# Class words of a graph network kernel: 10 of 25 groups in the setup, 15 one a step, and a loop that begins at step 19

## The reference

```
A1 = adj * (y @ y.T)                      # edges within one class
x  = layernorm(x + 0.9 * (A1 / rowsum(A1)) @ x + 0.1 * h0)
w  = tanh(adj * adj), the 350 largest of each row kept
h2 = tanh(x @ W_proj + b_proj)
x  = layernorm(x + relu(w @ (h2 @ W_gcn) + b_gcn))
```

## Time and profile before

| what | us |
|---|---|
| three runs | 461.50, 460.99, 461.31; median 461.31 |
| the profiled execution | 461.15 |
| its span, first to last instruction | 459.4 |
| TensorE busy | 429.9 (94%) |
| VectorE busy | 379.3 (83%) |
| ScalarE busy | 266.5 (58%) |
| GpSimd busy | 162.2 (35%) |

### The profile page before, as it was taken

How to read it: one execution, slowest core, us unless ns; L and a number is a source line. 1 busy time by engine, 2 the same in 40 slices (tenths; PEclk the granted TensorE clock), 3 DMA queues, 4 the chain that set the end, 5 groups by cost and what they waited for, 6 DMA issues and landing times.

```text
span 459.4 us, 15106 instructions
## 1 busy us (share of the span) xinstructions
PE 429.9 (94%) x5104; PEld 381.6 (83%) x5104; DVE 379.3 (83%) x1363; ACT 266.5 (58%) x363; POOL 162.2 (35%) x311
## 2 busy tenths in 40 slices
PE   3669999999999999999999999999999999999994
PEld 2447998888988888888888987788888888888883
DVE  5988999999999999999999987786666666666663
ACT  4987999998999999999999963840000000000000
POOL 3012443544455544455544453132221221221222
PEclk9986999999999999999999999999999999999998
DMA  8999999999999999999999500000000000000000
GB/s 267 409 414 420 393 411 411 392 414 409 421 415 422 423 422 417 423 421 423 417 424 422 221 2 2 8 17 11 17 16 12 17 15 13 17 14 15 17 13 26
DMA packets 25518, 108.49 MB, mean 236 GB/s; under 512 B 5097, under 2 KB 15490, under 8 KB 15490
## 3 DMA queue, kind: packets, MB, share of 16 engines
q1 hardware_dynamic: 25490, 108.14, 58.4%
HBM read 105.57 MB, written 2.56 MB: 235 GB/s over the span
## 4 chain that ended last, share of the span: by engine, by line
PE 77%; DVE 10%; issue 6%; ACT 3%; DMA 2%; POOL 2%; POOLq 0%; DVEq 0%; SPq 0%
PE acc L576 65%; PE words L514 6%; DVE a_bits L862 3%; DMA a_rows<-in_adj_dram 2%; DVE turned L949 2%; PE feat_acc L643 2%; PE proj_acc L656 1%; PE xnt_acc L635 1%; ACT count_out L743 1%; ACT x_parts L729 1%; DVE z_high L1017 1%; POOL rstd L454 1%; DVE stats L1030 1%; DVE mean_var L1035 0%; DVE f_parts L982 0%
## 5 line engine op out<-in xcount | busy, mean ns | idle before, releaser
L576 PE MATMUL acc<-x_parts,turned 128*128 128x257 f16 x1560 | 189.2, 277 | 4.5 <-DVE turned L949 3.5
L743 ACT ACTIVATE count_out<-a_rows,ones 128x2688 bf16<-128x2688 f32 (+1 forms) x80 | 190.2, 2377 | 0.5
L576 PEld LDWEIGHTS acc<-x_parts,turned 128*128 128x128 fp8e4 x1560 | 152.3, 99 | 27.3 <-issue 4.9
L576 PE MATMUL acc<-f_parts,turned 128*128 128x256 f16 x1520 | 165.3, 271 | 1.8 <-DVE f_parts L982 1.8
L576 PEld LDWEIGHTS acc<-f_parts,turned 128*128 128x128 fp8e4 x1520 | 147.1, 98 | 18.9 <-DVE f_parts L982 1.3
L862 DVE TENSOR_SCALAR a_bits<-a_rows 128x2688 bf16<-128x2688 f32 (+1 forms) x80 | 116.6, 1457 | 1.9 <-DMA a_rows<-in_adj_dram 1.5
L451 POOL TENSOR_TENSOR var_eps<-mean_var,consts 128x1 f32<-128x1 f32 x79 | 18.4, 233 | 258.5 <-DVE mean_var L1035 129.6
L949 DVE TENSOR_SCALAR turned<-a_words 128x320 uint16 (+1 forms) x304 | 66.2, 231 | 48.7 <-PE acc L576 48.7
L454 POOL TENSOR_TENSOR rstd<-var_eps,consts 128x1 f32<-128x1 f32 x79 | 87.3, 1105 | 6.2
L949 DVE TENSOR_SCALAR turned<-same_class 128x320 uint16<-128x320 uint16 x313 | 71.4, 254 | 0.1
L514 PEld LDWEIGHTS words<-pack,a_bits 128*128 128x128 bf16 (+1 forms) x1600 | 51.6, 97 | 9.5 <-DVE a_bits L862 7.5
(11 more groups left out here) (134 smaller groups left out, 295.6 us busy)
## 6 DMA issues: line engine op xcount, KB each, us to landing
a_rows<-in_adj_dram SPq DMA_DIRECT2D x39, 1344.0 KB, 7.5
a_rows<-in_adj_dram SPq DMA_DIRECT2D x39, 1156.0 KB, 8.0
out_dram<-xn SPq DMA_DIRECT2D x39, 64.0 KB, 1.5
h_rows<-in_L_gnn_h_dram SPq DMA_DIRECT2D x19, 128.0 KB, 7.7
xs<-in_x_dram SPq DMA_DIRECT2D x3, 640.0 KB, 10.0
xs<-in_x_dram SPq DMA_DIRECT2D x1, 512.0 KB, 9.0
y_nat<-in_L_gnn_y_dram SPq DMA_DIRECT2D x1, 304.0 KB, 3.6
a_rows<-in_adj_dram SPq DMA_DIRECT2D x1, 84.0 KB
```

The source lines that it names most:

```text
L576: mm = pe.matmul(acc[par][0:m, used], bits, parts[:, b, used], start=first and b == blocks[0], stop=last and b == blocks[-1])
L743: act.activation(count_out[0:m, 0:w], a_rows[par][h][0:m, 0:w], ACT.Relu, bias=ones[0:m, 0:1], scale=-HUGE, accum_out=col).then_inc(s_coun ...
```

## The change

Groups 10 to 14 leave step 1 (on TensorE, ScalarE and VectorE). Groups 10 to 24 are made one a step in steps 2 to 16 instead of groups 15 to 24 in steps 2 to 11. Since group g is now made in step g - 8, VectorE copies the even groups in steps 2, 4, ..., 16 and ScalarE the odd ones in steps 4, 6, ..., 16. `FIRST` becomes 19, so that steps 13 to 18 are written out. Two waits are new: TensorE's transpose of step 5 waits for the copies of groups 6 to 9, whose banks it shares, and `mask` of block 16 waits for groups 13 and 14.

```diff
-    FIRST = 13
+    FIRST = 19
...
-        EARLY_GRAMS = 3 * GRAMS
+        EARLY_GRAMS = 2 * GRAMS
...
                 same_class_words(0)
-                if not started and t == 1:
-                    for g in range(2 * GRAMS, 3 * GRAMS):
-                        gram_words(g)
                 if valid(t - 5):
                     m5 = rows_of(t - 5)
                     if isinstance(t, int) and t == 5:
                         pe.wait_ge(s_const, 9)
+                        for g in range(EARLY_GRAMS - 4, EARLY_GRAMS):
+                            pe.wait_ge(*gram_copied(g))
...
-                if isinstance(t, int) and t == 1:
-                    for g in range(2 * GRAMS, 3 * GRAMS):
-                        if not gram_on_dve(g):
-                            copy_words(g)
...
-                if isinstance(n, int) and (n in (0, PART) or n == FIRST - 2):
+                if isinstance(n, int) and (n in (0, PART, 2 * PART) or n == FIRST - 2):
...
                 if t == 1:
                     cast(1, 1, 0, 0)
-                    copy_words(10)
-                    copy_words(12)
                     cast(1, 1, 0, 1)
-                    copy_words(14)
```

## The result

| | before | after |
|---|---|---|
| median of 7 runs, us | 460.92 (459.84 to 461.50) | 462.56 (462.17 to 464.25) |
| ratio of the runs | | 1.0044 [1.0028, 1.0061] |
| profiled execution, its span | 461.15, 459.4 | 462.17, 460.4 |
| step 3 begins on VectorE | 37.00 | 35.96 |
| step 19 begins | 139.44 | 139.48 |

The changed kernel is slower by 0.44%, 2 us. The forecast was 462.2 with a range of 460.3 to 463.2. A step "begins" here with its first cast on VectorE.

What follows compares the result with a forecast made beforehand. DMA was taken to bound up to about 43 us, then VectorE's instruction list to the matrix's end. Terms 0, -0.1, -0.3 and +1.33 gave +0.9 us on 461.15; with 0.16 to the median, 462.2, range 460.3 to 463.2.

Steps and rivals of the forecast that it cites:

- Part 1: Step 1 made lighter: VectorE's cast of half 1 starts about 2 us sooner, but DMA binds, so worth 0.
- Part 2: Steps 2 and 3: step 2's added copy fits idle time, step 3 loses its copy; -0.1 us, bounds 0 and 0.6.
- Part 3: Steps 4 to 9: three VectorE copies before and after, but one more step behind a copy; -0.3 us.
- Part 4: Steps 10 to 18: VectorE copies in 10, 12, 14 and 16 instead of one in step 11; 58.11 against 56.78, +1.33 us.
- The return behind a copy: On VectorE, a step behind one with a copy is 0.2 to 0.3 us shorter, through GpSimd's power operation.
- the loop from step 19 on: Loop behind the written-out steps: no cost of its own; step 19 begins 0.9 us later and the end shifts by as much.
- Written-out steps are cheaper: Rival for steps 13 to 18: loop overhead of 0.42 us a pair vanishes, giving +0.2 us, 461.5; chance 0.2.
- The start isn't bound by DMA: Rival for steps 2 and 3: sooner loads land sooner, removing 1.52 us of waits; 460.7 or 460.0; chance 0.15.
- Full price: Rival for steps 10 to 18: three extra copies at 0.60 us, nothing returned behind them; +1.8 us, 463.1; chance 0.12.
- DMA bounds the written-out steps: Rival for the written-out steps: DMA moves less there, six steps take 0.25 us more each; 463.2; chance 0.08.

Runs made afterwards that it cites:

- second pair of profiles: One further profile each of the unchanged kernel before and the unchanged changed kernel; measured 460.24 and 461.76 us.
- e4: Changed kernel with 81 semaphore increments in VectorE's list during setup, putting the loop at place 639; 462.62 us, ratio 1.0038.
- e10: Changed kernel without VectorE's eight copies in steps 2 to 16, leaving out the class condition from block 8 on; 461.07 us, ratio 0.9988.
- e3: Kernel before with one more semaphore increment at the start of VectorE's list, loop at place 384; 460.59 us, ratio 0.9992.
- e5: Kernel before with row statistics moved ahead of the cast of half 1 and moments right behind it on VectorE; 458.91 us, ratio 0.9947.
- e7: Kernel before with steps 13 to 36 written out (FIRST 37), leaving one loop iteration; 462.22 us, ratio 1.0033.
- e1: Kernel before with steps 13 to 18 written out too (FIRST 19), groups where they were; 461.34 us, ratio 1.0003.
- e8: Kernel before, unchanged, profiled once more (also called before again); 460.24 us.

## Why the prediction was right, and where it wasn't

The direction, the engine and the likeliest mechanism were right; the size was 0.9 us where the runs show 1.6 to 2.0. That the forecast time, 462.2, is only 0.4 from the measured 462.56 is partly luck: it was counted from 461.31, the median of three runs of before, and seven runs give 460.92.

- **Part 1, the start, priced at 0: right.** Its working was off: 27.73 - 28.94 has the wrong sign, and the cast of half 1 ends 3.2 us sooner (27.10 against 30.29), not 2. But DMA makes nothing of it: in the second pair of profiles the last piece of step 2's rows lands at 29.74 before and 29.75 after, that of step 3's at 35.71 and 35.76. Taken as they stand, the two first profiles show step 3 a whole microsecond earlier. That is no effect of the change: before again has 35.74, and of the other kernels most lie between 35.72 and 36.01, e4 at 36.52 for its increments, e10 at 36.63, and e3, a kernel before, at 37.15. The prediction's own test for this step ("wrong, if step 3 begins earlier") was thus badly set: one profile can't carry it.
- **Part 2, -0.1.** Step 3 takes 5.95 instead of 6.13: -0.18.
- **Part 3, -0.3.** Steps 4 to 9 take 39.06 (41.91 to 80.97 [after]) instead of 39.53: -0.47.
- **Part 4, +1.33.** Steps 10 to 18 take 58.51 instead of 56.78: +1.73. The terms were 6.91 with a copy, 6.04 behind one, 6.31 for step 18; measured are 6.94 to 6.96, 6.21, 6.04, 6.09, 6.03, and 6.34. The measured sum is 0.4 above the forecast one since most terms were some hundredths short, and step 11's alone 0.17. Together parts 2 to 4 give +1.08 against +0.93, so the copies' price stood as a whole. The return behind a copy is as forecast; its reason, that the power operation's 1.90 us is 0.55 plus the rest of the cast, comes to 2.04 by the rows (the cast ends at 90.25), and e5 shows that the step gets shorter by when the power operation's result is there, even if it still takes 1.7 to 1.9 us.
- **The failed term: the loop from step 19 on, in the sum at 0.** It costs +0.85 (125.58 against 124.73): nine jumps with 2.02 us in all instead of 1.21 give 0.81 of it. The prediction took code that isn't edited for code that isn't changed. It did have the reverse thought, a branch that vanishes when a step is written out, but not that the remaining branches could change their price.
- **Rivals.** "Written-out steps are cheaper" is refuted by e7 and e1: they are dearer by 0.03 to 0.07 us a step (the forecast had them 0.03 cheaper). "The start isn't bound by DMA" is refuted: what is won in step 1 reappears as a wait of 2.71 us for the rows, and they land no sooner. "Full price" is refuted by 6.03 to 6.09 behind three of the four copies (step 11, with 6.21, is just over its line of 6.2) and by e10's 0.32 a copy in steps 10 to 13. "DMA bounds the written-out steps" is refuted for this kernel, 417 GB/s between 45 and 100 us without a wait; it is the next bound, as e5 and e10 show.
- **Adding up.** From step 3 to step 39 the change costs 229.10 - 227.17 = 1.93 us, and 1.47 in the second pair of profiles; the medians differ by 1.64, and the ratio makes it 2.0. With the first profiles' difference of 1.04 at the start it comes to the 0.89 at step 39, which would have seemed to confirm the +0.9 for a wrong reason.

## What to carry to other kernels

An instruction moved into the bounding engine's list costs its busy time less what the neighbours give back, and that share has to be read from steps with and without it: here it cost 0.32 us of 0.60 in four steps, and 0.44 to 0.57 on the mean of twelve. If the number of written-out steps is changed, the unchanged loop behind them has to be compared as well, iteration by iteration. And before a shift of a microsecond at the start is explained, a second profile of the same kernel should show that it stays.

## What the runs showed of the hardware

- **The price of a jump on VectorE depends on where the loop stands.** Places 383 and 384: 0.134 us; 558 and 559: 0.218; 441: 0.233; 639, which is 383 + 256: 0.134 again, twice. The second layer's loop follows: 0.113 at 675 and at 931, 0.260 at 850 and again at 1362 (e7), which is 850 + 512, and 0.134 at 733. There it costs nothing: an iteration takes 8.63 us at 0.113 and at 0.260 alike. ScalarE's first loop went the other way, from 0.192 to 0.116, off the path. The Trainium skill (Runtime: NRT & Kernel Launch, section Instruction fetch mechanics) gives 256 instructions as one block in which an engine's list is refilled. That the price returns after 256, and after 512 in e7, agrees with it; its long stall at a branch shows in no run. The rule for the places between stays open.
- **The start varies.** Step 3 begins at 35.7 to 36.0 in most profiles and near 37.1 in two, and before shows both with the same code. The mean rate in 24 to 38 us hardly differs (423 GB/s in e8, 420 in before). A load lands in 16 pieces, and the last one lags: of step 3's rows the 15th landed at 34.74 and the 16th at 36.98 in before, at 35.46 and 35.71 in e8. e3 (35.06 and 37.13) and e10 (34.83 and 36.61) are like before; why is open.
- **Loop iterations alternate.** In the loop a step takes 6.0 to 6.1 and the next, which ends with the jump, 6.43 to 6.54; written out most take 6.34. A pause on VectorE ahead of the cast, be it a copy or a jump, is partly given back by the next step, as the power operation on GpSimd gets ahead of the cast.
